# Mixture-of-experts kernel: the gathers at its end wait for TensorE one pair less far ahead, and the first token tile's gathers wait for fewer expert pages

## The reference

```python
def body(acc, ws):
    ew1, ew2, ew3, ce = ws
    h = jax.nn.silu(x @ ew1.T) * (x @ ew3.T)
    return (acc + ce[:, None] * (h @ ew2.T), None)
y, _ = jax.lax.scan(body, jnp.zeros_like(x), (w1, w2, w3, combine.T))
shared = jax.nn.silu(x @ sw1.T) * (x @ sw3.T) @ sw2.T
return (y + shared).reshape(B, S, H)
...
x = x + s * g
```

## Time and profile before

| | us |
|---|---|
| median of 3 runs | 686.68 |
| lowest and highest | 683.47, 690.63 |
| the profiled execution | 691.99 |
| its span | 690.2 |
| busy TensorE, VectorE, ScalarE, GpSimd | 548.6, 472.2, 359.1, 383.4 |

### The profile page before, as it was taken

One profiled execution on the slowest core, in us unless ns is written; L12 is line 12 of the kernel. 1 busy time (PEld: TensorE's weight loads), 2 busy tenths in 40 slices (PEclk: granted clock), 3 DMA queues, 4 the chain that ended last, 5 costly groups with the idle time before them and its releaser, 6 DMA issues.

```text
span 690.2 us, 14473 instructions
## 1 busy us (share of the span) xinstructions
PE 548.6 (79%) x4095; PEld 446.7 (65%) x4095; DVE 472.2 (68%) x1443; ACT 359.1 (52%) x606; POOL 383.4 (56%) x402
## 2 busy tenths in 40 slices
PE   7789696979697978437999889888888889888830
PEld 6566575756576765326999777777777777677620
DVE  6968687877788877722454567667677667667765
ACT  5546464546464644224655656556556556556421
POOL 1156667676666766753003556556565556565662
PEclk9889798998898999868999999999999999999975
DMA  9999996858393532754888888888888988888764
GB/s 320 416 354 347 366 334 227 285 214 298 130 334 113 207 117 91 230 150 122 201 217 262 290 280 283 280 280 285 290 272 292 279 279 267 290 276 286 226 198 141
DMA packets 111288, 174.80 MB, mean 253 GB/s; under 512 B 25072, under 2 KB 68848, under 8 KB 110320
## 3 DMA queue, kind: packets, MB, share of 16 engines
q1 hardware_dynamic: 87280, 108.29, 47.4%
q0 software_dynamic: 18432, 50.36, 23.2%
q10 hardware_dynamic: 5504, 15.24, 6.4%
HBM read 78.41 MB, written 92.27 MB: 247 GB/s over the span
## 4 chain that ended last, share of the span: by engine, by line
PE 53%; DVE 21%; issue 15%; another core or an unknown queue 6%; ACT 4%; DMA 1%; DVEq 0%; SPq 0%; ACTq 0%
PE ps L835 17%; PE ps L857 8%; PE ps L726 7%; PE ps L710 6%; PE ps L818 6%; PE ps L718 4%; DVE sw L1133 3%; PE ps L845 3%; PE ps L732 2%; DVE w_all L1050 2%; DVE work L1152 2%; DVE work L1159 1%; DVE stats L877 1%; DVE early L1141 1%
## 5 line engine op out<-in xcount | busy, mean ns | idle before, releaser
L508 POOL DMA_INDIRECT early<-slots_d,slot_at x192 | 186.6, 972 | 178.0 <-DMA slots_d<-early 56.6
L487 POOL DMA_INDIRECT slots_d<-early,slot_at x96 | 96.9, 1009 | 75.0 <-issue 25.7
L487 POOL DMA_INDIRECT slots_d<-work,slot_at x96 | 97.7, 1018 | 45.1 <-issue 26.5
L835 PE MATMUL ps<-w_all,xnT 128*128 x798 | 102.9, 275 | 15.9 <-issue 13.6
L835 PEld LDWEIGHTS ps<-w_all,xnT 128*128 128x128 f16 x798 | 71.4, 98 | 36.3 <-issue 24.6
L647 ACT ACTIVATE xnT<-ps 128x1024 f16<-128x1024 f16 x67 | 68.8, 1029 | 46.6 <-PE ps L818 28.0
L668 ACT ACTIVATE early<-ps 128x512 f32<-128x512 f32 x112 | 67.3, 602 | 46.6 <-remote 30.8
L818 PE MATMUL ps<-ident,work 128*128 128x128 f16 x796 | 66.7, 222 | 24.9 <-issue 24.8
L1159 DVE CAST work<-ps 128x256 f16<-128x256 f32 x75 | 31.6, 422 | 75.0 <-remote 45.0
L1133 DVE SCALAR_TENSOR_TENSOR sw<-early,wk,sw 128x256 f32<-128x256 f32 x160 | 77.7, 486 | 3.5
L818 PEld LDWEIGHTS ps<-ident,work 128*128 128x128 f16 x796 | 54.6, 99 | 28.8 <-issue 26.4
(11 more groups left out here) (164 smaller groups left out, 989.4 us busy)
## 6 DMA issues: line engine op xcount, KB each, us to landing
slots_d<-early SPq DMA_DIRECT2D x112, 256.0 KB
work<-slots_d SPq DMA_DIRECT2D x100, 256.0 KB
slots_d<-pad SPq DMA_DIRECT2D x7, 3072.0 KB
w_all<-in_wexp ACTq DMA_DIRECT2D x7, 1536.0 KB
slots_d<-work SPq DMA_DIRECT2D x1, 5120.0 KB, 19.2
s_all<-in_x SPq DMA_DIRECT2D x8, 512.0 KB, 6.3
ysh_d<-work ACTq DMA_DIRECT2D x8, 512.0 KB
early<-ysh_d SPq DMA_DIRECT2D x32, 128.0 KB
```

Of the source, the lines that this page charges most:

```text
L487: pool.indirect_dma_start(slots_d[:, :], bass.IndirectOffsetOnAxis(ap=slot_at[:, at:at + 1], axis=0), split[b % XN_RING][:, t, :], None).t ...
L508: pool.indirect_dma_start(gath[:, at % GATH_RING, :], None, slots_d[:, :], bass.IndirectOffsetOnAxis(ap=slot_at[:, rank_of(at):rank_of(at) ...
L835: mm = pe.matmul(ps[:, 5 + p % 2, h * 2 * I:(h + 1) * 2 * I], turned_x(p)[:, x_low * HC + k, h * P:(h + 1) * P], w16[:, bass.ds(at + (w_lo ...
```

## The change

Two expressions in GpSimd's loop change. `pages` is the number of pages from the front of `slots_d` that gather `at` may reach. It was `at + 32` for all; for the six gathers of the first token tile it is now `at + 27`, so they wait for the stores of fewer pairs. The pair of TensorE that is waited for is now counted from the last pair that must be stored: `complete + 4` in place of `at // 2 + 21`.

```diff
             for at in range(GATHERS):
-                pages = at + E
+                pages = at + E - (TOP_K - 1 if at < TOP_K else 0)
                 complete = min(-(-pages // 2), PAIRS)
                 for pair in range(stored, complete):
                     pool.wait_ge(s_store[pair % DEEP], 16 * (pair // DEEP + 1))
                 stored = complete
                 if at >= GATH_RING:
                     pool.wait_ge(s_acc, at - GATH_RING + 1)
-                ahead = at // 2 + 18 + SOON
+                ahead = complete + 1 + SOON
                 if at % 2 == 0:
                     pool.wait_ge(s_ehT_ps, min(ahead, PAIRS))
                 else:
                     pool.wait_ge(s_eT_ps, turns(min(ahead + SOON + 1, PAIRS - 1)))
```

## The result

| | before | after |
|---|---|---|
| median | 688.33 us | 694.3 us |
| lowest and highest of 20 runs each | 683.15, 692.53 | 689.87, 699.64 |
| the profiled execution, its span | 691.99, 690.2 | 698.62, 696.9 |

The ratio of after to before is 1.009 (95% interval 1.006 to 1.0119). The forecast was 685.5 us, in a range of 679 to 691: the time went the other way and lies outside the range. The ratio is within 1%, to which the prediction gave 0.79. Of the 8.8 us between 685.5 and 694.3, 1.65 are the start from three runs (686.68) where 20 give 688.33; the change's own part is +6.0 where -1.2 was forecast.

The account below looks back on a forecast made before the run. The second stage was taken as bound by the turn of four gathers and TensorE's late results. Terms -0.8, +0.9 and -1.3 sum to -1.2 us, from the median 686.68 to 685.5 us; range 679 to 691.

Parts of the forecast that it names:

- What bounds the kernel: Second stage: bound by a 6.57 us turn, four gathers (4.84 us) plus 1.74 us until GpSimd hears of TensorE.
- The first six gathers: Start of the gathers: going early, nearly one behind the other, they cost one group of four less what is saved, +0.9 us.
- The even gathers from 6 on: Middle: their changed wait mostly doesn't bind, the odd gathers' does; 14 groups save 0.06 us each, -0.8 us.
- The last gathers: End: gather 178 starts at 659.5 against 660.84 before, later gathers and the end follow, -1.3 us.
- That sign that the sum would be wrong: End: the wait before the eviction of pair 110 not lying between 5 and 13 us.
- Rival 1: Whole kernel: nothing changes, as even waits don't bind and the rings take up the early gathers; 686.7 us, chance 0.28.
- Rival 2: Second stage: groups grow to five or six gathers, 0.04 us less a gather; 679.2 us, chance 0.12.
- Rival 3: Second stage: groups shrink to two and GpSimd pays the 1.74 us twice as often; 706.5 us, chance 0.06.
- Rival 4: Start: early gathers collide with SyncE's loads, seven TensorE steps cost 0.65 us each, 4.6 us; 689.2 us, chance 0.07.
- What the profile would show: GpSimd: L845 waits nearly gone, L818 waits above 24, sum near 65 us; groups of four, each opened by an odd gather.
- The step that lengthens before 379: Start of the gathers: TensorE's steps lengthening before 379 us, named as a sign that the sum would be wrong.

Follow-up runs that it names:

- the repeat: The whole change run again in a later session against the kernel before, giving a second trace: 694.54 against 688.09 us, 1.0106.
- the first six alone: Kernel before with only the first six gathers' closer page bound and earlier TensorE wait, all as before from gather 6 on: 698.26 us, 1.0026.
- the spread six: Kernel before with the closer page bound for the first six gathers, each waiting for one turn_hidden more than the one before: 696.11 us, 1.0.

## Why the prediction was wrong

**What bounds the kernel**: the reading held, in sessions of the 688 kind (the turn of four stands in those of the 696 kind, too). The stage is bound by the turn of gathers and late results; without the gathers no step of TensorE is over 2.7 us, and the kernel is 60 us faster (one run). "Over 50 us" was the prediction's figure for it.

**The first six gathers** (term +0.9 us, bounds -0.4 to +2.6) are the step that failed. Their start was right (3.0 us behind turn_hidden(17) by the forecast's 364.5; 4.4 and 3.4 in two traces), the row of six was right (done by 372 forecast, 372.94 measured; five and one in the repeat), and the mechanism, too. The size was not: they cost 4.87 us, and 3.79 in the repeat. Two choices in the step were wrong. I took "one group of four", when I had myself worked out that the six go nearly one behind the other; and I priced a row in proportion to the middle's turn. There TensorE has lost 1.3 us for two steps because the next group is held back until results come through. In one row of six nothing comes through for 7.2 us, nearly three steps, while the rings hold two or three. Even the upper bound, two full groups (2.6 us), was built that way. The sum to make was another: 7.22 us of issuing and 1.37 us until the results are through are 8.6 us, less what the rings cover. But that part is known only afterwards and isn't fixed: 3.7 us here (8.6 - 4.87), and for the rows of five (6.0 us, and 1.2 or 1.3 until the results are through) 3.4 in the repeat and 5.0 in the first six alone. Why the same row cost 3.79 us in one and 2.32 in the other stays open.

**The even gathers from 6 on** (-0.8 us, bounds 0 to -0.8) had the wrong sign, by little. The pace of odd gathers is what binds, as said, and the waits for L845 fell from 14 to 8. But the fall brought nothing: alone the edit is 1.0021. In the whole it lets fours form right behind the first six, where there were twos without it; the prediction looked at gather 82 only, and not at which waits the edit frees at gathers 6 to 15. That the twos would have made the kernel faster isn't shown: the spread six have them and take the time of before.

**The last gathers** (-1.3 us, bounds -5.3 to +2.7) measured -1.22 and -1.66 from pair 110 to the end, and that is luck. Counted from pair 102 they are -1.3 and +0.9. The way there was another, too: a row of nine and one of eleven, not one that begins at 178, and the eviction of pair 110 waited 0.68 us, not the 5 to 13 of the forecast, since the late results fell on pair 106 (109 in the repeat). That sign that the sum would be wrong, which I called the likeliest, came.

**The rivals.** Rival 1 (nothing) is what the 590 kind shows, for a reason that it didn't have. Rival 2 (groups grow): two groups of six were in the middle, with 1.60 us a gather as forecast, but the turns beside them took up to 9.14 us. (Its price was added up wrong: 180 gathers at 0.04 us are 7.2 us and not 7.5.) Rival 3 (groups shrink) didn't come. Rival 4 had the place and nearly the price (4.6 us in seven steps against 4.87), but not the cause: it blamed the loads, and the spread six, with the same gathers as early and a higher DMA share, cost nothing. Its 0.07 was too little, since the price of a full stall at that place belonged into the term's own bounds, whatever its cause.

**What the profile would show**: the L818 waits rose from 24 to 29 as forecast, and the sum of both was 69.1 us (65 forecast). The waits for L845 aren't nearly gone. The step that lengthens before 379 was named as a sign that the sum would be wrong, and it was that.

**What stays open.** Of the loss of 6.0 us (median) the start holds 4.9 and the end may give back 1.2. The rest, some 2 us in each trace, lies between the pairs 66 and 102 in one and 102 and 110 in the repeat; with one trace of the kernel before, scatter can't be told from effect there. That groups of six cost anything isn't shown either, since the spread six have one and the time of before. The parts' ratios in the session of the 696 kind add up to 0.47%, 3.3 us, about half of what the whole loses in those of the 688 kind (6.0 and 6.5 us). Whether the parts make each other worse, or cost less in that session, stays open.

## What to carry to other kernels

Where a profile shows results arriving only after a row of DMA issues ends, price an edit by its longest unbroken row against the depth of the rings, not by the mean cost of a group: five or six in a row cost TensorE 2.3 to 4.9 us at that place where the same six, spread over nine microseconds, cost it nothing. A wait that seems not to bind in the middle of a loop can still be what keeps issues apart at its start. A change that works on such a stall should be timed in more than one session. And a stretch of one trace that comes out as forecast proves little: move the cut by a few steps and see whether it stands.

## What the runs showed of the hardware

**Indirect DMAs in a row hold TensorE's results back from the other engines** in sessions of the 688 kind, and cost 60 us there; the turn of four gathers, 6.6 us, is in the traces of the 696 kind, too. Plain DMAs of the same size issued by GpSimd cost nothing that one run can show (623.7 us against 628.51 without any); issued by SyncE it was 635.75. A plain DMA's row on GpSimd is 0.54 us where the gather's is 0.95. What about the gathers holds the results wasn't settled: the form, the unbroken row or the scattered reads. Quarter-size gathers, which would tell the issue from the transfer, weren't tried.

**The same program took 589.7, 688.09 and 696.49 us** in different sessions. In those of the 590 kind the hold isn't seen: 96 gathers in one row beside a TensorE that is busy 100.00 of 100.00 us. The granted clock in that window is 1.00 in both, so it isn't TensorE's clock. The first stage is shorter there, too: the first turn_hidden starts at 278.14 us in place of 321.69, which is 43.6 of the 102.7 us between the two traces, and without any gathers the kernel still takes 584.77 us in one kind and 628.51 in the other. Two windows, 0 to 300, of before in the 688 kind and of the changed kernel in the 590 kind, the granted clock 0.89 and 0.93:

```profile
0.00:300.00 300.00, 234.84 (x1056) 180.51 (x1057) 228.71 (x844) 156.08 (x247) 184.01 (x199) 0.89 0.74 257
```

```profile
0.00:300.00 300.00, 255.20 (x1349) 201.46 (x1350) 242.76 (x883) 174.70 (x278) 194.80 (x210) 0.93 0.82 277
```

GpSimd has only indirect scatters in that stage. Whether they hold results in the same way there, or the sessions differ in something more, stays open, and so does what makes a session one kind or the other.
